# Mamba block with routed FFN on one core: statistics of z on ScalarE in two passes, and another share of the C products on VectorE

## The reference

```python
def _layernorm(x, axis=-1, eps=1e-05):
    m = jnp.mean(x, axis=axis, keepdims=True)
    v = jnp.var(x, axis=axis, keepdims=True)
    return (x - m) / jnp.sqrt(v + eps)
...
def step(state, xs):
    d_t, B_t, C_t, u_t = xs
    dA = jnp.exp(d_t[..., None] * A)
    state = state * dA + (d_t * u_t)[..., None] * B_t[:, None, :]
    y_t = jnp.einsum('ben,bn->be', state, C_t)
    return (state, y_t)
...
y = y + D[None, :, None] * u
y = y * jax.nn.silu(z)
...
x = x + jnp.tanh(g_xattn[0]) * _L0_xattn_ref(ctx_1024, _layernorm(x, axis=-1), ...)
x = x + jnp.tanh(g_ffn[0]) * _L0_ffn_ref(_layernorm(x, axis=-1), ...)
```

## Time and profile before

| | us |
|---|---|
| median of 3 runs | 533.96 |
| lowest, highest | 533.24, 534.74 |
| profiled execution, own time | 533.53 |
| its span, first to last instruction | 531.8 |
| PE busy | 491.4 (92% of the span) |
| DVE busy | 462.9 (87%) |
| POOL busy | 451.9 (85%) |
| ACT busy | 380.1 (71%) |

### The profile page before, as it was taken

One profiled execution on the slowest core, in us unless ns is written; L12 is line 12 of the kernel. 1 busy time (PEld: TensorE's weight loads), 2 busy tenths in 40 slices (PEclk: granted clock), 3 DMA queues, 4 the chain that ended last, 5 costly groups with the idle time before them and its releaser, 6 DMA issues.

```text
span 531.8 us, 9178 instructions
## 1 busy us (share of the span) xinstructions
PE 491.4 (92%) x3018; PEld 368.0 (69%) x3018; DVE 462.9 (87%) x846; ACT 380.1 (71%) x699; POOL 451.9 (85%) x327
## 2 busy tenths in 40 slices
PE   9989899998787999999999999999899999899688
PEld 5568788687676676668676777767566766676654
DVE  3799799799799999799999999798988989999852
ACT  4698848775876777866958776957868869768542
POOL 1389999959999999989999999889799898888910
PEclk9969799999999999999999999999999999999899
DMA  5595000126520001065230000077100000000001
GB/s 127 176 375 217 0 2 1 41 85 213 182 80 1 1 1 60 1 229 202 71 101 2 20 1 22 8 281 227 45 21 1 22 20 17 6 21 21 2 20 39
DMA packets 18704, 39.36 MB, mean 74 GB/s; under 512 B 5585, under 2 KB 6353, under 8 KB 18658
## 3 DMA queue, kind: packets, MB, share of 16 engines
q1 hardware_dynamic: 18658, 38.79, 21.4%
HBM read 34.33 MB, written 4.46 MB: 73 GB/s over the span
## 4 chain that ended last, share of the span: by engine, by line
PE 48%; POOL 19%; DVE 13%; ACT 10%; issue 9%; DMA 1%; DVEq 0%; SPq 0%; POOLq 0%; ACTq 0%
PE p_s L759 12%; PE p_y L781 11%; POOL state L586 9%; POOL dbu L571 7%; DVE state L1267 6%; PE p_v L814 5%; PE p_f L805 5%; PE p_tr L728 3%; PE p_v L691 2%; ACT da L1016 2%; DVE x L1216 2%; PE p_pr L703 2%; ACT pair_b L1000 1%; PE p_f L794 1%; PE p_pr L682 1%
## 5 line engine op out<-in xcount | busy, mean ns | idle before, releaser
L586 POOL TENSOR_TENSOR state<-state,c_bc 128x1024 f32<-128x1024 f32 (+1 forms) x131 | 256.7, 1970 | 21.6 <-DVE state L1267 19.2
L759 PEld LDWEIGHTS p_s<-pair_b,du_t 128*128 128x128 f32 x1072 | 140.7, 200 | 44.9 <-issue 33.4
L759 PE MATMUL p_s<-pair_b,du_t 128*128 128x128 f32 x1072 | 154.6, 287 | 16.0 <-DVE state L1267 15.8
L781 PE MATMUL p_y<-ident,state 128*128 128x128 f32 x1024 | 149.3, 276 | 0.0
L1016 ACT ACTIVATE p_s<-delta,a_neg 128x512 f32<-128x512 f32 (+1 forms) x162 | 93.7, 583 | 77.6 <-DVE state L1267 44.1
L1267 DVE TENSOR_TENSOR_SCAN state<-da,p_s 128x512 f32<-128x512 f32 (+1 forms) x116 | 134.5, 1172 | 16.0 <-PE p_s L759 13.1
L571 POOL TENSOR_TENSOR dbu<-du,pair_b 128x1024 f32<-128x1024 f32 (+1 forms) x80 | 145.3, 1819 | 0.2 <-DMA pair_b<-bc_rows 0.2
L781 PEld LDWEIGHTS p_y<-ident,state 128*128 128x128 f32 x1024 | 121.5, 144 | 23.3 <-issue 20.2
L1016 ACT ACTIVATE da<-delta,a_neg 128x512 f32<-128x512 f32 (+1 forms) x158 | 99.3, 647 | 18.5 <-DVE state L1267 18.4
L1267 DVE TENSOR_TENSOR_SCAN state<-p_s,dbu 128x512 f32<-128x512 f32 (+1 forms) x100 | 97.6, 996 | 7.6 <-POOL dbu L571 6.0
L805 PE MATMUL p_f<-u_sb,h_t 128*128 128x512 f32 x112 | 55.4, 597 | 2.4 <-DVE gw L1364 2.4
(11 more groups left out here) (175 smaller groups left out, 640.6 us busy)
## 6 DMA issues: line engine op xcount, KB each, us to landing
c_bc<-bc_rows SPq DMA_DIRECT2D x32, 512.0 KB, 5.1
pair_b<-bc_rows SPq DMA_DIRECT2D x16, 512.0 KB, 5.5
xs<-in_x SPq DMA_DIRECT2D x16, 256.0 KB, 4.6
out<-ot SPq DMA_DIRECT2D x14, 256.0 KB, 2.0
cx<-in_ctx_t SPq DMA_DIRECT2D x4, 512.0 KB, 3.8
u_sb<-in_u_w SPq DMA_DIRECT2D x1, 1024.0 KB, 14.1
v_sb<-in_v_w SPq DMA_DIRECT2D x1, 1024.0 KB, 15.6
w_in<-in_in_w_t SPq DMA_DIRECT2D x1, 384.0 KB, 4.7
```

What stands on the lines that cost most here:

```text
L586: eng.tensor_tensor(pair, pair, c_bc[:, 2 * p:2 * p + 2, c0:c0 + w], ALU.mult).then_inc(po_cs, 1)
L759: mm = eng.matmul(p_s[g % BANKS][:, t * P:(t + 1) * P], du_t[:, f % 2, t, :], diagonals_of(n // 2)[:, n % 2, c0 // P + t, :], start=(t == ...
L781: mm = eng.matmul(p_y[:, t, :], slot(NS * f + n)[:, t * P:(t + 1) * P], ident[:, :], is_transpose=True, start=False, stop=(n == NS - 1 and ...
```

## The change

Statistics of z. For blocks 4 to 15 DVE's two instructions go. ACT does it with three: a Copy of the block with the sum as accumulator output, the sum times -1/512, and a Square of the block less its mean, again with the sum. They stand behind the decays of n = 11, 12 and 13 of phases 0 to 11; the one of n = 12 comes after `conv_first`. POOL's `scale_of_z` for batches 1 to 3 has three operations in place of four, and stands in the batch's first phase instead of the last phase of the batch before. Blocks 0 to 3 stay as they were.

C products. Pair 1 goes from POOL to DVE in phases 1 and 2, and from DVE to POOL in phase 3. Pair 5 goes to DVE in 4, 6, 8 and 10 and to POOL in 3. Six pairs go to DVE, two to POOL.

```diff
     PAIRS_BY_DVE += [(f, p) for f in range(SPLIT, F) for p in (1, 4)]
-    PAIRS_BY_DVE += [(f, 1) for f in range(Q - 1, SPLIT)] + [(f, 5) for f in range(Q - 1, SPLIT, Q)]
+    PAIRS_BY_DVE += [(f, 1) for f in range(1, SPLIT) if f != 3] + [(f, 5) for f in (4, 6, 7, 8, 10, 11)]
...
             def scale_of_z(b):
-                eng.wait_ge(ve_zs, 2 * Q * (b + 1))
-                if b >= 2:
-                    eng.wait_ge(ac_z, Q * (b - 1))
+                if b:
+                    eng.wait_ge(ac_zs, 3 * Q * b)
+                    if b >= 2:
+                        eng.wait_ge(ac_z, Q * (b - 1))
+                    eng.tensor_scalar(zv[:, 0, :], z_of[:, 2, :], 1.0 / E, EPS, ALU.mult, ALU.add).then_inc(po_zs, 1)
+                    eng.wait_ge(po_zs, zops(b - 1) + 1)
+                    eng.tensor_tensor(zr[:, b % 2, 0, :], zv[:, 0, :], minus_half[:, :], ALU.pow).then_inc(po_zs, 1)
+                    eng.wait_ge(po_zs, zops(b - 1) + 2)
+                    eng.tensor_tensor(zr[:, b % 2, 1, :], z_of[:, 1, :], zr[:, b % 2, 0, :], ALU.mult).then_inc(po_zs, 1)
+                    return
...
+                if k == 0 and b and c0 == 0:
+                    scale_of_z(b)
                 times_c(f, 1)
...
                 if turning:
-                    scale_of_z(b + 1)
                     diagonals(b + 1, 1)
...
+            def z_statistics(q, part):
+                b, k = q // Q, q % Q
+                if part == 0:
+                    eng.wait_ge(s_x[b % 2][k], 16 * (b // 2 + 1))
+                    eng.wait_ge(ve_dl, q - Q + 2)
+                    if b > 1:
+                        eng.wait_ge(po_zs, zops(b - 1))
+                    eng.activation(vsp[:, :], xs[:, b % 2, k, :], ACT.Copy,
+                                   accum_out=z_of[:, 0, k:k + 1]).then_inc(ac_zs, 1)
+                elif part == 1:
+                    eng.wait_ge(ac_zs, 3 * (q - Q) + 1)
+                    eng.activation(z_of[:, 1, k:k + 1], z_of[:, 0, k:k + 1], ACT.Copy, scale=-1.0 / E).then_inc(ac_zs, 1)
+                else:
+                    eng.wait_ge(ac_zs, 3 * (q - Q) + 2)
+                    eng.activation(vsp[:, :], xs[:, b % 2, k, :], ACT.Square, bias=z_of[:, 1, k:k + 1],
+                                   accum_out=z_of[:, 2, k:k + 1]).then_inc(ac_zs, 1)
...
                     if n == 12 and f + 5 < BLOCKS:
                         conv_first(f + 5)
+                    if n in (11, 12, 13) and f + Q < BLOCKS:
+                        z_statistics(f + Q, n - 11)
...
-                    if n == (1 if f % Q else 14) and f + Q < BLOCKS:
-                        z_statistics(f + Q)
```

More of the change, by code:

```diff
@@ L204, in flamingo @@
         zv = sb("zv", [P, 2, Q])
+        z_of = sb("z_of", [P, 3, Q])
         zr = sb("zr", [P, 2, 2, Q])
@@ L277, in flamingo @@
         ac_h = sem("act_h")
+        ac_zs = sem("act_z_statistics")
         ac_e = sem("act_exp_scores")
@@ L368, in broadcasts_of_b, with zops @@
             return sum(p in pool_pairs(a) for a in range(b + 1)) + (p == 0)
-        ZOPS = 4
+        def zops(b):
+            return 4 + 3 * b
         FOPS = 3
@@ L588, in scale_of_z @@
             def scale_of_z(b):
-                eng.wait_ge(ve_zs, 2 * Q * (b + 1))
-                if b >= 2:
-                    eng.wait_ge(ac_z, Q * (b - 1))
+                if b:
[8 more added lines that the diff above has]
+                    return
+                eng.wait_ge(ve_zs, 2 * Q)
                 eng.tensor_tensor(zv[:, 0, :], zmv[:, :, 1], eps_c[:, :], ALU.add).then_inc(po_zs, 1)
-                eng.wait_ge(po_zs, ZOPS * b + 1)
+                eng.wait_ge(po_zs, 1)
                 eng.tensor_tensor(zr[:, b % 2, 0, :], zv[:, 0, :], minus_half[:, :], ALU.pow).then_inc(po_zs, 1)
-                eng.wait_ge(po_zs, ZOPS * b + 2)
+                eng.wait_ge(po_zs, 2)
                 eng.tensor_tensor(zv[:, 1, :], zmv[:, :, 0], zr[:, b % 2, 0, :], ALU.mult).then_inc(po_zs, 1)
-                eng.wait_ge(po_zs, ZOPS * b + 3)
+                eng.wait_ge(po_zs, 3)
                 eng.tensor_tensor(zr[:, b % 2, 1, :], zv[:, 1, :], minus_one[:, :], ALU.mult).then_inc(po_zs, 1)
@@ L1025, in skip @@
                                scale=dsk[:, k:k + 1]).then_inc(ac_skip, 1)
+            def z_statistics(q, part):
[14 more added lines that the diff above has]
+                                   accum_out=z_of[:, 2, k:k + 1]).then_inc(ac_zs, 1)
             def silu_z(f):
                 b, k, c0, w = PHASE[f]
-                eng.wait_ge(po_zs, ZOPS * (b + 1))
+                eng.wait_ge(po_zs, zops(b))
                 eng.wait_ge(s_x[b % 2][k], 16 * (b // 2 + 1))
@@ L1229, in z_statistics @@
             def z_statistics(q):
-                b, k = q // Q, q % Q
-                eng.wait_ge(s_x[b % 2][k], 16 * (b // 2 + 1))
+                eng.wait_ge(s_x[0][q], 16)
                 if q:
                     eng.wait_ge(ve_zs, 2 * q)
-                eng.bn_stats(zst[:, :], xs[:, b % 2, k, :]).then_inc(ve_zs, 1)
+                eng.bn_stats(zst[:, :], xs[:, 0, q, :]).then_inc(ve_zs, 1)
                 eng.wait_ge(ve_zs, 2 * q + 1)
-                if b:
-                    eng.wait_ge(po_zs, ZOPS * b)
-                eng.bn_aggr(zmv[:, k, :], zst[:, :]).then_inc(ve_zs, 1)
+                eng.bn_aggr(zmv[:, q, :], zst[:, :]).then_inc(ve_zs, 1)
             def scan(f, n):
```

## The result

The change ran at a median of 543.03 us (542.85 to 544.51, 4 runs) against 533.6 us for the kernel before beside it (532.96 to 534.74, 4 runs): ratio 1.018, 95% interval 1.0155 to 1.0206. It is slower. The profiled execution took 542.85 us, its span 541.1 us against 531.8.

The account below looks back on a forecast made before the run. No single engine bounds the kernel: DVE and POOL fill phase 5, PE phase 7, all three nearly phase 10. Terms 1.3 + 4.0 + 5.0 - 0.8 = 9.5 us on 533.53 gave 543.0 us, range 536.5 to 548.

Parts of the forecast that it names:

- Phases 1 and 2, +1.3: Phases 1 and 2: PE gets the bank of n = 6 later, 0.6 and 0.7 us, together +1.3 us.
- the two pairs that come cost little: Phase 3: the two pairs moved to POOL cost little, because POOL waits there for scans.
- The first stop, 5.3 us long, +4.0: Phase 4: ACT's copy waits for x's load, DVE stops 5.3 us; PE is 4.0 us late in phase 7.
- a tap late by 4 us or more: Phase 4: DVE's first convolution tap comes 4 us or more late; otherwise the forecast is wrong.
- phase 4 longer by 4 to 6 us: Profile after the change: phases 4 and 8 each get longer by 4 to 6 us.
- the rival with 0.13: Phases 4 to 6: POOL sets the pace, only 1.5 us of the first stop comes out; 537 to 540 us, chance 0.13.
- The second stop, 4.6 us long, +5.0: Phase 8: ACT's copy waits for x's load, DVE stops 4.6 us; PE's next waits move by 5.0 us.
- Phases 9 to 11, -0.8: Phases 9 to 11: two short PE waits may give back 0.8 us, between 0 and 1.7.
- scale_of_z "only moves", 0: POOL's scale_of_z keeps its power and moves a few steps later, at a cost of 0.
- Phases 12 to 19, 0: Phases 12 to 19: untouched except for the moved scale_of_z, so 0.
- The clock rival, 0.10: After PE's phase 8 wait its clock stays at 1.2 GHz, adding 2 to 3 us: 545 to 546 us, chance 0.10.
- Phase 7 "as long as before": Profile after the change: phase 7, where PE is the bound, keeps its length.

Follow-up runs that it names:

- kernel with late statistics and phase 3's pairs on DVE: Changed kernel with ACT's z statistics in phases 4 and 8 moved behind the decays of n = 14 and 15, phase 3's pairs on DVE: 533.59 us, ratio 0.999.
- statistics alone: Changed kernel with the C products shared as before the change, z statistics on ACT kept: 538.23 us, ratio 1.0085.

## Why the prediction was right, and where it was not

The forecast of 543.0 us was met, and the mechanism that carried it, the stop behind the copy, is shown by the runs. But the sum came out partly because errors cancel. Term by term:

- **Phases 1 and 2, +1.3**: +1.4 by the starts of du. The four kernels with the old pairs in these phases are at -0.2 to -0.7 there. DVE's milestone of phase 2 has +1.2, and PE's clock was at 0.50 in phase 1 both before and after, so the two can be compared. Right.
- **Phase 3, "the two pairs that come cost little"**: a step that failed. Window 3 itself got 0.9 us shorter, but window 4 got 2.2 longer, and the two pairs together cost 2.8 us. I had looked at POOL's waits in phase 3 and had taken them as room for both pairs. They are room for the first only. The second stands at 128.85, past the last idle time, on the way to the terms of phase 4. DVE in the changed kernel gets no later there (+1.0 in phase 3, +1.1 in phase 4), because another term that I had at nothing cancels it: scale_of_z no longer stands ahead of the same terms.
- **What comes back where nothing stops**: the sum had nothing for it ahead of phase 9. The kernel with late statistics and phase 3's pairs on DVE goes from +1.3 in phase 3 to -0.8 in phase 7: some 2 us come back, 1.8 of them in phase 4, most of which is scale_of_z.
- **The first stop, 5.3 us long, +4.0**: mis-sized. The load landed after 2.9 us, not 4.9, and DVE stood for 3.26 us. Its price is 1 to 2.8 us. The stated sign, a tap late by 4 us or more, appeared (4.44), yet 1.1 us of it was not the stop: DVE's scan behind POOL's term was already that late (144.97 against 143.87). A sign that adds two causes can't confirm one of them. The other sign, phase 4 longer by 4 to 6 us, failed: it is 2.2 us by POOL's windows and 2.8 by DVE's milestones.
- **What of it would be absorbed**: the rival with 0.13. In this place it is partly right: DVE's milestone goes from +1.1 in phase 4 to +3.9 in phase 5 and is back at +2.6 in phase 6. That POOL set the pace there, as the rival has it, is not shown; DVE and POOL had both lost work.
- **The second stop, 4.6 us long, +5.0**: landing 4.6, ACT idle for 4.41, DVE for 5.55, PE for 4.15. Price 4.5 and 4.8 by the ratios, 4.4 and 5.1 by the starts. Right.
- **Phases 9 to 11, -0.8**: nothing came back; behind the second stop the starts go from +7.5 to +7.7, and DVE stays at +8.4.
- **scale_of_z "only moves", 0**: right in sum, not in detail. In phase 12 the move costs nothing that DVE's milestone shows, and in phase 4 it gives 1.6 to 1.8 us. My 0 holds for this gain and the cost of phase 3's pairs together, and for neither alone.
- **Phases 12 to 19, 0**: +0.3 up to phase 18, and 0.6 behind it, in which PE's clock was low for longer. In the profiled executions of nine further kernels phase 18's du to the end took 46.4 to 47.6 us at a mean clock of 0.93, and in two others and before 46.0 to 46.2 at 0.96. What decides it was not tried.
- **The clock rival, 0.10**: the clock did fall to 0.50 after the 4.15 us of PE's wait, and was there still in the window from 282. A price on top of the stop doesn't show: DVE's tap waited 5.55 us where it had waited 0.44, which alone is 5.1, and the stop's price is 4.4 to 5.1. No run took the two apart. The 0.6 us at the end are a price of the clock that no rival had.
- **Phase 7 "as long as before"**: 29.90 against 29.25 us, with PE full in both.

In short: forecast 1.3 + 0 + 4.0 + 5.0 - 0.8 + 0 = 9.5. Measured by DVE's milestones: 1.2 up to phase 2, -0.1 from there to phase 4, 1.7 from phase 4 to 8 with the first stop in it, 5.6 from 8 to 9, 0 in 9 to 12, 0.3 up to phase 19, 0.6 behind, 9.3 in all. The overrated first stop paid for the 0.8 us that didn't come back, for 0.6 more at the second stop, and for the 0.9 behind phase 12; and the C products of phase 3, which I had at nothing, were paid by the move of scale_of_z, which I had at nothing too. That the total fits to 0.2 us is luck; that the second stop carries half of it is not.

## What to carry to other kernels

When a cheap instruction with a wait for a load is put on an in-order engine, cost what stands behind it, not the instruction: look for the next operation in that list that another full engine needs, and put the waiting one behind it; one slot was worth 7.5 us here. Before an engine's idle time is spent on added work, find the last idle time ahead of the next consumer, since work added after it is late in full. And where several small terms were set to zero by "it only moves" or "there is room", a total that fits doesn't show that they were zero: read the lateness from milestone to milestone, and on two engines, since a step on one engine alone can be the loss of a lead.

## What was not expected of the hardware

- The same load of four blocks of 256 KB, sent by SP in phase 4, had its first block there after 4.9 us before and 2.9 in the changed kernel. In the other eleven it took 2.5 to 3.0 us in nine, 4.0 and 4.1 in two. In phase 8 the first block took 3.6 to 4.6 us in all thirteen. The Trainium skill, page DMA: Bandwidth & Descriptors, section Anatomy of one DMA, gives by its fit for another issue path an estimate of 2.6 us for 256 KB: ten of the phase 4 landings agree to 0.4 us, the rest and those of phase 8 are 1 to 2.3 us over. What makes the difference was not tried. The forecast had taken its 4.9 us from the slowest of the thirteen, so a single landing time is good to 2 us at best.
- A stop that an engine passes on is not passed on at its own length. 1.33 us of ACT's waiting (statistics alone, phase 4) cost 0 to 1.6 us, 3.42 us cost 1 to 2.8, 4.41 us cost 4.4 to 5.1. The two last differ in length by a third and in price by more: around the first DVE and POOL had work taken off them, and behind the second PE is full, as the earlier trace rows show for phase 10. Which of these made the difference was not tried.
- PE's clock makes one and the same program's executions differ. In phase 1 the same list of instructions, with PE idle for 1.67 us in one execution and 1.68 in the other, ran at 1.00 in the one and fell to 0.50 in the other, and DVE was 1.4 us apart behind it (-1.9 and -0.4). So a difference of 1 us in a start, taken from one execution of each kernel, can be the clock alone.
